# A decoder layer on one core: the group loop of its attention and routing part in a new order on four engines

## What is computed

```
x = ln(x + attn(x))                    # attn has three residual steps of its own
x = ln(x + xattn(x, ctx, mask))
x = ln(x + ffn(x))

attn:  gamma = softplus(ln1(x) @ w_pot) + 0.1
       x += bk_diag(...) @ w_bk + b_bk                # continued fractions
       q, k, v = ln2(x) @ w_qkv                       # 8 heads of 64
       x += hebbian(q, k, v, gamma) @ w_out           # linear attention with decay
       x += gelu_tanh(ln3(x) @ w_ff1) @ w_ff2
xattn: softmax(q k^T / sqrt(8) - 100 * mask) @ v @ Wo # 16 heads of 8
ffn:   logits = x @ Wr; two best of 8 experts, weights renormalised
       out = sum of w_e * (gelu_erf(x @ W1[e]) @ W2[e])
```

## Time and profile before

| | before |
|---|---|
| runs, us | 838.68, 839.81, 839.96 (median 839.81) |
| profiled execution, us | 841.11, its span 839.2 |
| mean granted clock of TensorE | 0.916 |
| PE busy | 667.1 us, 79% |
| DVE busy | 547.5 us, 65% |
| ACT busy | 400.7 us, 48% |
| POOL busy | 346.7 us, 41% |
| part of the eight groups | from about 114 to 638 us of the span |
| part of the experts | from about 655 to 807 us |

### The profile page before, as it was taken

The page is one execution under the profiler, slowest core; times in us unless marked ns, Lnnn a source line. Parts: engine busy times, 40 slices in busy tenths (PEclk is TensorE's granted clock), DMA queues, the critical chain, the costliest instruction groups (busy, mean ns, idle before and its releaser), DMA issues.

```text
span 839.2 us, 20345 instructions
## 1 busy us (share of the span) xinstructions
PE 667.1 (79%) x6207; PEld 483.2 (58%) x6207; DVE 547.5 (65%) x1768; ACT 400.7 (48%) x860; POOL 346.7 (41%) x503
## 2 busy tenths in 40 slices
PE   5325788988988888989899899899892799999930
PEld 1212454754664665574575485485472799989930
DVE  3594557766765875874965865865876366656644
ACT  2001144546536536537436537445542477767726
POOL 2534056065155246245344425425416154544435
PEclk9555989999999999999999999999997799999975
DMA  7600000000000000000000000000023222222144
GB/s 250 217 0 14 0 21 21 2 8 26 6 0 29 10 0 26 13 0 23 16 0 19 19 0 19 19 0 19 19 100 78 63 63 73 67 66 65 56 169 151
DMA packets 32108, 36.68 MB, mean 44 GB/s; under 512 B 9690, under 2 KB 24987, under 8 KB 31808
## 3 DMA queue, kind: packets, MB, share of 16 engines
q1 hardware_dynamic: 23872, 23.09, 9.0%
q0 software_dynamic: 4608, 9.59, 3.4%
q10 hardware_dynamic: 3584, 3.48, 1.2%
HBM read 23.35 MB, written 12.76 MB: 43 GB/s over the span
## 4 chain that ended last, share of the span: by engine, by line
PE 50%; DVE 22%; issue 11%; POOL 7%; ACT 3%; DMA 3%; DVEq 2%; SPq 0%; POOLq 0%; ACTq 0%
PE bank L1465 13%; PE bank L1748 6%; PE bank L1758 5%; PE bank L1505 4%; DVE negmax L1140 3%; POOL rstd L728 3%; PE bank L1626 3%; PE bank L1553 2%; PE bank L1561 2%; PE bank L1595 2%; DVE xn L1025 2%; DVE stats L1016 2%; PE bank L1613 2%; PE bank L1634 2%; DVE x L1129 2%
## 5 line engine op out<-in xcount | busy, mean ns | idle before, releaser
L725 POOL TENSOR_SCALAR vare<-mv 128x1 f32<-128x1 f32 (+1 forms) x113 | 24.6, 218 | 287.5 <-DVE mv L1021 287.5
L642 ACT ACTIVATE hT<-bank,qT 128x128 f32<-128x128 f32 x288 | 82.1, 368 | 54.1 <-PE bank L1748 54.1
L829 POOL DMA_INDIRECT expert_out<-xa,v_sb x72 | 70.9, 985 | 87.4 <-DVE xa L1347 60.4
L1748 PE MATMUL bank<-xnT,qT 128*128 128x128 f32 x576 | 81.9, 286 | 2.3 <-DVE qT L1333 1.5
L770 POOL DMA_INDIRECT expert_in<-xb_rows,slot_u x72 | 72.5, 1007 | 21.2 <-issue 17.4
L1140 DVE TENSOR_REDUCE negmax<-bank 128x4 f32<-128x512 f32 x128 | 79.3, 681 | 2.7 <-PE bank L1595 2.7
L533 ACT ACTIVATE mix<-bank 128x512 f32<-128x512 f32 x128 | 66.1, 603 | 28.7 <-PE bank L1613 27.9
L1758 PE MATMUL bank<-w_t,hT 128*128 x576 | 76.9, 277 | 0.6 <-DVE xa L1340 0.5
L1748 PEld LDWEIGHTS bank<-xnT,qT 128*128 128x128 f32 x576 | 71.5, 195 | 8.2 <-DVE qT L1333 2.9
L728 POOL TENSOR_TENSOR rstd<-vare,minus_half 128x1 f32<-128x1 f32 (+1 forms) x113 | 70.5, 624 | 10.1 <-POOL vare L725 1.6
L1465 PE MATMUL bank<-xqT,w_qkv 128*128 128x512 f32 x144 | 72.3, 627 | 0.8 <-DVE kT L1053 0.8
(11 more groups left out here) (290 smaller groups left out, 1454.4 us busy)
## 6 DMA issues: line engine op xcount, KB each, us to landing
v_sb<-expert_in SPq DMA_DIRECT2D x72, 66.0 KB
ctxT<-in_ctxT SPq DMA_DIRECT2D x9, 256.0 KB, 2.9
w_t<-in_w_t ACTq DMA_DIRECT2D x1, 2064.0 KB, 8.2
xT_all<-in_xT SPq DMA_DIRECT2D x4, 512.0 KB, 5.6
x_all<-in_x SPq DMA_DIRECT2D x4, 512.0 KB, 9.0
w_t<-in_w_t SPq DMA_DIRECT2D x1, 2048.0 KB, 7.5
mix<-expert_out SPq DMA_DIRECT2D x4, 512.0 KB, 5.0
x_all<-expert_out SPq DMA_DIRECT2D x4, 512.0 KB, 8.2
```

Of the source, the lines that this page charges most:

```text
L642: ins = nc.scalar.activation(hx[j % 2][:, c, :], bank[2 + j % 2][:, c * P:(c + 1) * P], ACT.Gelu, bias=w1c[j % 2][:, FF + c:FF + c + 1])
L829: nc.gpsimd.indirect_dma_start(ys[:, :], bass.IndirectOffsetOnAxis(ap=tag[j % ROWS][:, HOME - P:HOME - P + 1].bitcast(U32), axis=0), ysb[j ...
L1748: ins = mm(bank[2 + j % 2][:, c * P:(c + 1) * P], w1c[j % 2][:, c * P:(c + 1) * P], xtT[j % 2], start=True, stop=True)
```

## The change

It moves instructions in the loop, changes nothing in what is computed and adds one small activation per group. The bank table is new: only its first lines are shown here, since its rows say nothing by themselves.

```diff
 JOBS = (
-    "ff1c0 ff1c1 ff1c2 ff1c3 xh2T ks0 ks1 ks2 ks3 ff2t0 ff2t1 ff2t2 ff2t3 decay q0 xaT k0 q1 k1 qf q2 "
+    "ff1c0 ff1c1 ff1c2 ff1c3 ks0 ks1 ks2 ks3 xh2T ff2t0 ff2t1 ff2t2 ff2t3 decay k0 q0 xaT q1 qf k1 q2 "
...
@@ ScalarE, group loop
                 drain(g, "xaT", xnT[:, :])
                 keys(g, 0)
                 queries(g, 1)
+                queries_high(g)
                 keys(g, 1)
-                queries_high(g)
                 queries(g, 2)
-                keys(g, 2)
                 placed_queries(g, 0)
...
                 drain(g, "xbT", xnT[:, :])
+                nc.scalar.activation(act_warm[:, :], minus_half[:, 0:1], ACT.Gelu_apprx_tanh)
                 act.wait_ge(xn_ready[LNB], ln_nth(g, T - 1) + 1)
...
                 nc.scalar.activation(ratio[:, :], below[:, :], ACT.Exp).then_inc(ratio_ready, 1)
+                drain(g, "xh3T", xnT[:, :])
                 keys_high(g)
                 context_values(g)
-                drain(g, "xh3T", xnT[:, :])
@@ GpSimd, prelude and group loop
             ln_scale(LN2, 1, 0, T)
-            heb_residual(1)
 
             with pool.Fori(0, G) as g:
+                first_sum_in(g + 2)
+                row_out(0)
+                heb_residual(g + 1)
                 gammas(g + 1)
-                row_out(0)
-                first_sum_in(g + 2)
                 ln_scale(LNA, g, 0)
...
-                ln_scale(LN2, g + 2, 0, T)
-                row_out(1)
                 pool.wait_ge(xn_ready[LNA], ln_nth(g, T - 1) + 1)
                 nc.gpsimd.tensor_tensor(
                     xab[:, :, :], xa[:, :, :],
                     bo_bc[:, :].unsqueeze(1).broadcast_to([P, T, P]), ALU.add).then_inc(xab_ready, 1)
+                ln_scale(LN2, g + 2, 0, T)
+                row_out(1)
                 row_out(2)
...
                 group_sum(g + 1)
-                heb_residual(g + 2)
+                pool.wait_ge(chosen_ready, g + 1)
                 pool.wait_ge(slot_ready, g + 1)
@@ VectorE, group loop
                 placed_queries(g, 3)
-                next_norm()
+                keys(g, 2)
                 maxima(0)
...
                 heb_sum(g, g + 1, 0)
                 decayed(g, 3)
-                heb_norm(g + 1, 0)
                 dve.wait_ge(xab_ready, g + 1)
...
                 heb_sum(g, g + 1, 1)
+                heb_norm(g + 1, 0)
                 dve.wait_ge(xb_free, g + 1)
...
                     ins = nc.vector.max_index(top_i[:, t, :], top8[:, t, :], lg[:, t, :])
                 ins.then_inc(route_link, 1)
+                heb_norm(g + 1, 3)
                 dve.wait_ge(route_link, g * 6 + 2)
...
                                         ).then_inc(chosen_ready, 1)
-                heb_norm(g + 1, 3)
...
                 nc.vector.tensor_copy(slot_u[:, :, :], slot_f[:, :, :]).then_inc(slot_ready, 1)
+                next_norm()
@@ TensorE, group loop
-                turn(g, "xh2T", LN2, g + 1, xn2)
                 place_keys(g)
+                turn(g, "xh2T", LN2, g + 1, xn2)
...
                 decays(g, g + 1)
+                keys(g, 0)
                 queries(g, 0)
                 turn(g, "xaT", LNA, g, xa)
-                keys(g, 0)
                 queries(g, 1)
-                keys(g, 1)
                 drained(pe, g, "xaT")
                 wide(g, "qf", wq_t[:, :], xnT[:, :])
+                keys(g, 1)
                 queries(g, 2)
+                place_queries(g)
                 keys(g, 2)
-                place_queries(g)
                 max_scores(0)
-                keys(g, 3)
                 queries(g, 3)
                 values(g, 0)
+                keys(g, 3)
                 turn_max(0)
...
                 turn_context(3)
+                heb_out(g, 0)
                 weigh(g, 1)
-                heb_out(g, 0)
-                scores(g, 3)
                 b = take(pe, g, "cxT")
...
                 done(ins, "cxT")
+                scores(g, 3)
...
-                turn(g, "xh3T", LN3, g + 1, xn, (6, 0, 0, 0))
+                turn(g, "xh3T", LN3, g + 1, xn)
```

More of the change, by code:

```diff
@@ L70 @@
 NB = 8
-BANK = dict(zip(JOBS, map(int, ("20174523061505462136103254236140537621075432105671430567346021753416752013456214"
-                            "17245062176306451735204"))))
+BANK = dict(zip(JOBS, map(int, ("76145237646505246103134502746105437261075432145671430567346021753416752013456214"
+                            "17254206176306451035274"))))
 NTH = {name: sum(BANK[m] == BANK[name] for m in JOBS[:n]) for n, name in enumerate(JOBS)}
@@ L158, in bass_decoder @@
         minus_half = sb("minus_half", [P, SEQS])
+        act_warm = sb("act_warm", [P, 1])
         gamma = sb("gamma", [P, SEQS + T])
@@ L1639, in _ @@
                     wide(g, f"ff1c{c}", w_ff1[:, tile(c)], xnT[:, :])
+                place_keys(g)
                 turn(g, "xh2T", LN2, g + 1, xn2)
-                place_keys(g)
                 for t in range(T):
```

2 lines of the change are left out of this document (1 added, 1 removed), and 4 rows, old and new, of the table JOBS.

## The result

The changed kernel took 806.0 us (median of 4 runs, 805.6 to 806.4), the kernel before on the same chip 839.9; the ratio is 0.960, with an interval of 0.958 to 0.961. The forecast was 822.6 with a range down to 811, so the gain of 33.9 us is twice the 17.2 that was forecast. The profiled execution took 806.3 us with a span of 804.5, against 841.1 and 839.2.

A forecast was written before the change was run, and what follows sets the result against it. Bound by PE's work plus a chain of waits through DVE, some held by GpSimd's sums. End -10.2, middle -6.0, `cxT` -0.8, eighth passage -0.2: -17.2 us from 841.11, median 1.3 lower, 822.6 us; range 811 to 833.

The forecast's parts named there:

- The end of a group: From `top_i` to the next `ff1`: without GpSimd's holds on DVE, `ff1` starts 1.45 us earlier, seven passages, -10.2 us.
- The middle: Between `qr` and the first maxima: four `xn2` norms leave, `k2` comes; -0.75 us per group, eight times, -6.0 us.
- the bound "1.2 earlier" for `low`: DVE's `low` in the middle: expected 0.1 us later under `xab`; bounds 1.2 earlier to 0.3 later.
- The constant matmuls: Six on PE (1.46 us) while it waits for the last `xn`: removal saves nothing by itself; clock effect a rival.
- `cxT` ahead of `scores(3)`: On PE: no 0.76 us idle for the drain, but `decayed(3)` waits longer; -0.1 us per group, -0.8 in all.
- The table loads: Two more on ACT after the drain of `xbT`: free with 0.9 us to spare, and they bring nothing.
- the bank table: PE's bank neighbours: only `mx2i0` gets a later drain ahead of it, over when PE comes; costed at nothing.
- GpSimd's queue: Start of a group: 1.26 us longer by `x1b`, first root 1.3 late, roots catch up within 0.3; taken as nothing.
- the rival that they hold ACT longer: The two new table loads each take 1.28 us more: 1.66 per passage, 11.6 in all, 834.2 us; chance 0.04.
- The clock: Falls at `ff1` and ahead of `mx0`: rival that less PE idling spares eight, -13.6 us, 809.0; chance 0.14.
- The slower rival: Without constant matmuls PE's clock falls earlier, staying low through `ff1`, `ks`, `ff2`; two more stretches per group give 849.8; chance 0.07.

The follow-up runs named there:

- the kernel with the old end and `xab` late: Changed kernel with `x1b` back at the group's end, last sequence's norm back behind `chosen`, and `xab` behind the LN2 roots: 824.9 us, ratio 0.977.
- the kernel with the old end: Changed kernel with `x1b` back behind `group_sum` at the group's end and the last sequence's norm back behind `chosen`: 858.3 us twice, ratios 1.019 and 1.017.

## Why the prediction was wrong

**The end of a group: right, a little small.** The reading that GpSimd's sums hold DVE's instructions was right at each place where it could be tested: the same cast took 0.16, 0.57 and 1.24 us by what ran beside it. Forecast 1.45 per passage, measured 1.56. The norm under `xf` ends 0.08 after the sum and not 0.35 after it, as `top_f` and `onehot` had shown in the earlier trace rows (0.05 and 0.09 after): a held instruction has done its own work by then, so its time is not added to the wait. That I added it made the path through the norm 0.27 too long. In return, `rank` waits 0.31 for `chosen`, which I had as just in time, and `ff1` starts 0.26 after ACT's drain is over (358.41) where I had 0.12. The two errors nearly cancel, which is luck.

**The middle: right in its parts.** Forecast -0.75 per group: `negmax` 0.85 earlier, `low` 0.1 later. Measured: `negmax` 1.05 earlier after `low`, and `low` 0.23 later after `ff1`, so -0.82. The run with the norms put back gives 0.80. The first sums were held for 1.01 us against the 1.28 expected; the bound "1.2 earlier" for `low` was out of reach even without `xab`: in the run with it moved away `low` comes 15.92 after `ff1`, 1.02 before the changed kernel and 0.79 before the kernel before (16.71 in a group without a fall at `ff1`). I had most of this chance in my own bounds and named it a cost of the change; it is the first thing to repair in it.

**The constant matmuls: wrong at "saves nothing by itself".** In the kernel before they cost nothing at the end (`below` to `ff1` 4.23 with and 4.22 without them), but in the changed kernel they cost 0.41 us per group. In the new order the first three transposes come at 356.3 and the fourth at 357.4, just behind its norm; with six constant matmuls (1.46 us) ahead of them all four come together, behind the norm. I costed them in the old order, and took them out of the new one.

**`cxT` ahead of `scores(3)`:** forecast -0.1, measured +0.08 per group by the periods. Both are small and the runs' times don't separate them, but the periods have the other sign.

**The table loads, the bank table, GpSimd's queue.** Table loads: nothing, as said, and with them falls the rival that they hold ACT longer. ACT waited 0.79 us behind them, the forecast's spare time was 0.9. The Trainium skill (ScalarE: Activation LUTs, "What ACT_TABLE_LOAD costs") would have added a drain of about 1.38 us to each; no row of the changed kernel shows one, since an activation starts 0.01 to 0.02 us after each load's 1.28. GpSimd's queue: taken as nothing, since it only matters in a group at full clock. With the clock spared, every group is one. The run with `x1b` at the end shows `low` 0.63 us sooner, which is what the longer queue costs, and which the change pays from what it gains.

**The clock: the step that failed.** The sum has no term for the clock; it takes the nine falls as staying. That is what made the prediction wrong: eight falls went, 12.0 us at 1.70 for those at `ff1` and 0.9 for those at `mx0`. The order alone, 22.7 us, would have given about 817, inside the range. I had the mechanism as a rival at 0.14, priced it at 13.6 and placed the time at 809.0. What spoke against it in my text was that busy time of PE would go there too with the constant matmuls. The two runs on them show that this was no argument: with or without them the clock falls nine times in the kernel before, and once in the changed kernel. The argument for it was in the numbers that I had: my own sum shortened the stretch from `below` to `ff1` by a third (4.2 to 2.8 us), a large change of what comes ahead of six of the nine falls. I should have given this case most of the chance, with 809 as its time; it would still have been 3 us high, since the order was worth 22.7 instead of 17.2 and the clock 12.0 instead of 13.6. Of its two reasons one holds: PE's waits ahead of `ff1` are shorter (1.2 us instead of 1.6), but in the middle most of the wait only moved, from `mx0` (0.44 left) to the placed queries (1.47).

**The slower rival** (more falls, 850 us) did not come with this change, nor when the constant matmuls alone were taken out of the kernel before (839.6 us, nine falls of the usual length). In part its mechanism is seen: in the kernel with the old end and `xab` late, without constant matmuls, three of the seven falls at `ff1` began earlier and lasted twice as long, and the first products took 6.3 to 6.7 us instead of 5.4. The 858 us of the kernel with the old end are no case of it, since with the constant matmuls it took 856.6, and the unexplained wait of the maxima is in both.

## What to carry to other kernels

Where VectorE and GpSimd both work on SBUF, look for small instructions that take a microsecond, and for the GpSimd instruction that ends as they do. Put GpSimd's large operations where VectorE's work is waited for by nobody. Count the falls of TensorE's clock one by one, with what each costs, before the sum of an edit is made: in this case an edit that shortened the stretch from `below` to `ff1` from 4.2 to 3.2 us or less gave back the falls there as well, and this must stand in the forecast and not beside it.

## What was not expected

Three runs with the old end and `xab` beside the first sums (one kernel twice, 858.3 us both times, and one with the constant matmuls, 856.6) had DVE's second maxima late by about 1.4 to 2.1 us in each group, with no releaser in the trace, on two chips. DVE's instructions up to there and PE's are the same, in the same order, as in the kernel with `x1b` alone at the end, which has no such wait; only the norm's place at the end of the group differs. In the group shown GpSimd issued scatters from 206.11 to 208.35, and the maxima started at 208.35. But the changed kernel has scatters at the same place beside its maxima (383.14 and 384.43, maxima at 383.23) and no wait, so a scatter beside them is not enough to hold them. Still, the late maxima keep step with GpSimd: in all 24 groups of the three runs they start either within 0.1 us of the end of the second of two scatters (15 groups) or about 0.2 us after its start (9 groups). Moving `xab`, which shifts the scatters by some 1.3 us, made it go away. What it is remains open.

A held instruction of VectorE ends with the GpSimd sum, whatever its own size. Over the kernels of this case a cast of 128x8 took 0.16, 0.57 or 1.24 us, a product of 128x64 0.23 or 1.25, one of 128x4 0.17 or 1.10, a norm of 128x128 0.33 or 0.74. Each long one ended within 0.1 us of a sum of 1.27 us. Not all are held: `max_index` kept its 0.16 us beside `xf` (356.57 above), and four `negmax`, which read PSUM, took 2.48 us beside `xab` (the changed kernel with it behind the LN2 roots) and 2.48 without it (318.84 above). The Trainium skill (SBUF — State Buffer, "Who interferes with whom") says that a VectorE instruction in a 2-port mode, or with two inputs in SBUF, contends with GpSimd for a shared pair of ports, that other VectorE instructions don't, and that the one that issues first "gets the shared pair for the whole instruction". The traces agree: 1.10 us for a product of 128x4, which has two inputs in SBUF, is the whole of what was left of the sum. Which of the held instructions with one input run in such a mode, no row shows.
